# Loading one half of the partitions from GpSimd, the other from SP

## The chip, the cores and the metric

The kernel runs on one core of one Trainium2 chip. The metric is device time in microseconds. Five engines work side by side: TensorE (PE), VectorE (DVE), ScalarE (ACT), GpSimd (POOL) and SyncE (SP). Each works its own list of instructions in order, and semaphores tie them together. DMAs are issued by an engine into a queue and carried out by 16 DMA engines.

## The reference

Two layers over 4096 nodes of 128 features, with one adjacency matrix `adj` of 4096 x 4096 fp32 (64 MB), which is read once in each layer:

```python
sim = jnp.tanh(adj * simlar)            # layer 0, simlar is adj: tanh(adj^2)
new_adj = ...                           # its 350 largest entries in each row
h2 = jnp.tanh(h @ W_proj + b_proj)
feat = jax.nn.relu(new_adj @ (h2 @ W_gcn) + b_gcn)
x = layernorm(x + feat)
pos = (adj > 0) @ x;  neg = (adj < 0) @ x       # layer 1
node = concat(pos, neg) @ node_weight + node_bias * diag(adj)
edge = (adj @ x) @ edge_weight + edge_bias * diag(adj)
x = layernorm(x + node + edge)
```

The matrix is sparse and has no negative entries. The kernel counts the positive entries of each row and the negative ones while it works; where no row has over 350 positive entries, the selection changes nothing, and a general path at the end (under `when_failed`) is skipped.

## The kernel before

Both layers go through the rows of `adj` in 8 chunks of 512 rows (`CHUNKS`, `CH`). A chunk is 8.39 MB. It is cut by columns into 4 pieces (`PIECES`), and a piece into 2 halves of 4 blocks each (`HALVES`, `HB`), so a chunk has 8 halves (`HPC`).

The 4096 columns are dealt to the partitions in quarters: partitions 0 to 31 hold columns 0 to 1023, partitions 32 to 63 the next 1024, and so on, each partition every 32nd row of the chunk. A piece is 256 columns of each quarter. So `load_chunk` (L309 to L321, on SP) issues four DMAs for a piece, one for each quarter. Each fills 32 partitions of `a_rows` with 16 x 256 numbers, that is 512 KB in 512 runs of 1 KB (L320). There are 4 slots in `a_rows`, one for each piece of a chunk; a slot is free for the next chunk's piece when VectorE has turned its second half (layer 0: `turned`), or when ScalarE has counted it (layer 1: `counted`). Before the chunks, SP loads x in 8 groups (L304), and after chunk 0's loads some small things, the diagonal of `adj` among them (L330).

The way of a half in layer 0:

- VectorE waits until the piece has landed and transposes each 32 x 32 square, `a_cols<-a_rows`, 128 x 2048 (`turn`, L477). `a_cols` has 4 slots for halves; a slot is free when TensorE has used it.
- GpSimd squares the first two blocks in place (L296), ScalarE the other two (L405); then ScalarE takes the tanh of all four (L409).
- TensorE multiplies the four blocks into the chunk's sum, `acc<-a_cols,rhs` (L874). An fp32 product stands as two records in the trace, so a half is 8 records and a chunk 64.

Behind this the chunk before is finished: ScalarE's relu (L394), VectorE's addition of x (L547), TensorE's turn of `z_t` into rows after half 1 (L839), VectorE's layer norm in three parts after its transposes 5, 6 and 7, TensorE's turn back of the new x after half 5 (L848), ScalarE's copy (L388).

In layer 1 the chunks run backwards from the last, which is still in `a_rows`. VectorE transposes a half and makes a mask of it (`masks<-a_cols`, L657); TensorE does three products for each block (L932 to L934); ScalarE goes over each piece in `a_rows` twice to count (L433, L436), and GpSimd has nothing. Results go out by DMAs that ScalarE issues, on another queue than SP's.

The order of each engine's work is written out by hand in the functions below; nothing reorders it. `chunks(engine, body)` (L214) runs a body for chunk 0, in a loop for the chunks 1 to 6, and for the last.

Of the kernel before, what the change touches and what calls it, by code (L numbers as in the profile page):

```python
# [21 lines left out]
SQ = 32  # L22
# [9 lines left out]
def build(nc, x, adj, w_proj, b_proj, w_gcn, b_gcn, node_w, node_b, edge_w, edge_b, out):  # L32
# [4 lines left out]
    QUARTERS = P // SQ  # L37
    QUARTER = N // QUARTERS
    BLOCKS = N // P
    CH = 512  # L40
    CHUNKS = N // CH
# [3 lines left out]
    PIECES = 4  # L45
    PCOLS = QUARTER // PIECES
    HALVES = 2
    HB = PCOLS // HALVES // SQ
    SLOTS = 4
    HSLOTS = 4  # L50
    HPC = PIECES * HALVES
    LAST = (CHUNKS - 1, CHUNKS // 2 - 1, 1)
    SQ_POOL = HB // 2

# [6 lines left out]
    with ctx:  # L61
# [6 lines left out]
        def sem(name):  # L68
            return ctx.enter_context(nc.semaphore(name))
# [7 lines left out]
        a_rows = sb("a_rows", [P, SLOTS, ROWSETS, PCOLS])  # L77
# [38 lines left out]
                     to_cols[:, 0:PARTS[1][1] * F].rearrange("p (t f) -> p t f", f=F)]  # L116


        def half_in(slot, h):
            w = PCOLS // HALVES  # L120
            return a_rows[:, slot, :, h * w:(h + 1) * w].rearrange("p r (b j) -> p r b j", j=SQ)
# [37 lines left out]
        x_loaded = [sem(f"x_loaded{g}") for g in range(CHUNKS)]  # L159
        small_loaded = sem("small_loaded")  # L160
        wl1_loaded = sem("wl1_loaded")
        a_loaded = [sem(f"a_loaded{k}") for k in range(SLOTS)]
        zeroed = sem("zeroed")
        consts = sem("consts")
        staged = sem("staged")
# [11 lines left out]
        counted = sem("counted")  # L177
# [34 lines left out]
        def chunks(eng, body):  # L212


            body((0, 0, 0), None)
            with eng.Fori(0, (CHUNKS - 2) // 2) as pair:
                body((pair * 2 + 1, pair, 1), (pair * 2, pair, 0))
                body((pair * 2 + 2, pair + 1, 0), (pair * 2 + 1, pair, 1))
            body(LAST, (CHUNKS - 2, CHUNKS // 2 - 1, 0))

        def rows_of(chunk):


            c, q, parity = chunk
            return c * -1 + (CHUNKS - 1), q * -1 + (QUARTERS - 1), 1 - parity
# [8 lines left out]
        EVEN_FIRST = [*range(0, GROUPS, 2), *range(1, GROUPS, 2)]  # L234
# [49 lines left out]
        @block.gpsimd  # L284
        def _(pool):
            nc.gpsimd.memset(ident[:], 0.0).then_inc(zeroed, 1)
            nc.gpsimd.memset(ones[:], 1.0).then_inc(consts, 1)
            pool.wait_ge(zeroed, 1)
            nc.gpsimd.affine_select(out=ident[:], in_=ident[:], compare_op=ALU.not_equal, fill=1.0, base=0,
                                    pattern=[[-1, P]], channel_multiplier=1).then_inc(consts, 1)  # L290

            def layer0(chunk, before):
                for h in range(HPC):
                    part = a_cols[:, h % HSLOTS, 0:SQ_POOL, :]
                    pool.wait_ge(turned[0], chunk[0] * HPC + h + 1)
                    nc.gpsimd.tensor_tensor(part, part, part, ALU.mult).then_inc(squared_pool, 1)  # L296

            chunks(pool, layer0)

        @block.sync  # L300
        def _(sp):
            def load_x():
                for g in EVEN_FIRST:
                    sp.dma_start(xr[:, g * TILES:(g + 1) * TILES, :],  # L304
                                 x[g * CH:(g + 1) * CH, :].rearrange("(t p) f -> p t f", p=P))\
                        .then_inc(x_loaded[g], 16)

            load_x()

            def load_chunk(layer, c):  # L310
                r = c * -1 + (CHUNKS - 1) if layer == 1 else c
                for s in range(PIECES):

                    if layer == 0 and not is_first(c):
                        sp.wait_ge(turned[0], HPC * (c - 1) + HALVES * (s + 1))
                    if layer == 1:
                        sp.wait_ge(counted, PIECES * (c - 1) + s + 1)
                    for q in range(QUARTERS):
                        src = adj[bass.ds(r * CH, CH), q * QUARTER + s * PCOLS:q * QUARTER + (s + 1) * PCOLS]
                        sp.dma_start(a_rows[SQ * q:SQ * (q + 1), s, :, :],  # L320
                                     src.rearrange("(r i) k -> i r k", i=SQ)).then_inc(a_loaded[s], 16)  # L321

            load_chunk(0, 0)

            for k, b in enumerate((node_b, edge_b, b_gcn)):
                sp.dma_start(b_row[:, k, :], b.rearrange("(a f) -> a f", a=1)).then_inc(wl1_loaded, 16)
            sp.dma_start(w_pne[:, 0:2, :], node_w.rearrange("(s p) f -> p s f", p=P)).then_inc(wl1_loaded, 16)
            sp.dma_start(w_pne[:, 2, :], edge_w).then_inc(wl1_loaded, 16)
            with nc.allow_non_contiguous_dma(reason="the diagonal"):
                sp.dma_start(diag[:], bass.AP(adj.tensor, 0, [[N + 1, P], [P * (N + 1), ALL_TILES]]))\  # L330
                    .then_inc(wl1_loaded, 16)

            for layer in range(2):
                with sp.Fori(1, CHUNKS) as c:
                    load_chunk(layer, c)

            sp.wait_ge(stored[0], 16 * (CHUNKS // 2))
            sp.wait_ge(stored[1], 16 * (CHUNKS // 2 + 1))

            with when_failed(sp):  # L340
                load_x()

                def g_load0(t, q, s):
                    sp.wait_ge(g_tile_free, t + 1)
                    sp.dma_start(g_in, adj[bass.ds(t * P, P), :]).then_inc(g_loaded[0], 16)
                    sp.dma_start(g_x, x[bass.ds(t * P, P), :]).then_inc(g_loaded[0], 16)

                def g_load1(t, q, s):
                    sp.wait_ge(g_tile_free, t + ALL_TILES + 1)
                    sp.dma_start(g_in, adj[bass.ds(t * P, P), :]).then_inc(g_loaded[1], 16)  # L350
                    sp.wait_ge(normed, t + NORMS + ALL_TILES + 1)
                    sp.dma_start(out[bass.ds(t * P, P), :], g_out).then_inc(g_stored, 16)

                g_tiles(sp, g_load0)
                g_tiles(sp, g_load1)
                sp.wait_ge(g_stored, 16 * ALL_TILES)
# [106 lines left out]
        def _(dve):  # L463
            EARLY = 3

            def turn(layer, c, h):

                s, hs = h // HALVES, h % HSLOTS
                n = c * HPC + h
                if h % HALVES == 0 and not (layer == 1 and is_first(c)):  # L470
                    dve.wait_ge(a_loaded[s], 16 * QUARTERS * (c + layer * (CHUNKS - 1) + 1))

                if h >= HSLOTS or not is_first(c):
                    dve.wait_ge(half_used[layer], n + 1 - HSLOTS)
                elif layer == 1:
                    dve.wait_ge(half_used[0], HPC * CHUNKS + n + 1 - HSLOTS)
                nc.vector.transpose(half_out(hs), half_in(s, h % HALVES)).then_inc(turned[layer], 1)  # L477
                return n, hs
# [579 lines left out]
```

## Time and profile before

| | |
|---|---|
| median of 3 runs | 723.9 us |
| lowest, highest | 722.14, 725.73 us |
| profiled execution, its span | 724.8 us |
| TensorE busy | 635.2 us, 88% |
| VectorE, ScalarE busy | 492.6 and 450.0 us, 68% and 62% |
| GpSimd busy | 122.2 us, 17% |
| moved by DMA | 130.62 MB, 180 GB/s over the span |

For the profiled execution the page gives its span alone; what lies around it shows in no view. The span is 0.9 us above the median of the runs.

The page cuts the span into 40 slices of 18.1 us. Slices 1 to 19 are layer 0 (until 353 us), the rest layer 1. Busy shares of an engine are averages over stretches with different limits, so they are to be read by stretch. In the rows by stretch each engine has its busy us and, in brackets, its instructions. A DMA share above 1 means that the packets' times overlap on a DMA engine. Lines such as L477 are lines of the kernel before; the change moves most of them by 10 or 26.

### The profile page before, as it was taken

Reading aid. Unit: us, or ns where it says so; the run is one execution under the profiler, and the core shown is the slowest. Engines: PE = TensorE matmul, PEld = TensorE weight load, DVE = VectorE, ACT = ScalarE, POOL = GpSimd, SP = SyncE. Lnnn points to the kernel's source line nnn. Section 1 sums busy time; section 2 is a strip of 40 time slices with the busy share of each in tenths; the row PEclk is TensorE's granted clock in tenths of the full one; section 3 lists DMA queues with packets and bytes.
Section 4 is the critical chain, followed back from the end, with each engine's and each line's share of the span. In section 5 each row is a group of like instructions: output and inputs, shape, how many; then the busy total and the mean of one; then the engine's idle time right before and its main releaser. Section 6 shows DMA issues by size and latency. Waiting matters only on the chain.

```text
span 724.8 us, 6808 instructions
## 1 busy us (share of the span) xinstructions
PE 635.2 (88%) x2016; PEld 353.6 (49%) x2016; DVE 492.6 (68%) x689; ACT 450.0 (62%) x302; POOL 122.2 (17%) x71
## 2 busy tenths in 40 slices
PE   7866858698786869696999999999999999999994
PEld 4522323243333334242666555555555555555993
DVE  3454574857656675748856489797978778787854
ACT  2564556565666655665318996768678667658750
POOL 0234334343334443334000000000000000000000
PEclk9998989989898989899899999999999999999998
DMA  9999999999999999993002999999999999999000
GB/s 208 214 176 209 212 211 212 212 212 211 211 211 212 211 212 212 211 213 73 1 0 54 212 211 211 226 213 227 213 227 212 227 213 212 226 212 220 16 16 16
DMA packets 140312, 130.62 MB, mean 180 GB/s; under 512 B 8579, under 2 KB 140294, under 8 KB 140294
## 3 DMA queue, kind: packets, MB, share of 16 engines
q1 hardware_dynamic: 135478, 128.16, 93.1%
q10 hardware_dynamic: 4816, 2.23, 1.2%
q8 instruction: 10, 0.16, 0.1%
q14 instruction: 8, 0.07, 0.0%
HBM read 128.27 MB, written 2.10 MB: 180 GB/s over the span
## 4 chain that ended last, share of the span: by engine, by line
PE 46%; SPq 42%; DMA 4%; issue 3%; DVE 3%; ACT 2%; DVEq 0%
SPq L320 40%; PE acc L932 23%; PE acc L934 6%; PE acc L933 6%; DMA a_rows<-in_adj_dram 4%; PE stage L896 2%; PE stage L952 2%; PE acc L952 2%; PE acc L874 1%; DVE a_cols L477 1%; ACT a_rows L436 1%; ACT a_rows L433 1%; SPq L304 1%; PE stage L954 1%; PE acc L954 1%
## 5 line engine op out<-in xcount | busy, mean ns | idle before, releaser
L477 DVE STREAM_TRANSPOSE a_cols<-a_rows 128x2048 f32<-128x2048 f32 x128 | 293.0, 2303 | 163.2 <-DMA a_rows<-in_adj_dram 124.3
L874 PE MATMUL acc<-a_cols,rhs 128*128 128x512 f32 x512 | 243.6, 633 | 21.3 <-ACT a_cols L409 21.3
L932 PE MATMUL acc<-a_cols,rhs 128*128 128x512 f32 x448 | 229.0, 592 | 0.0
L933 PE MATMUL acc<-masks,pos_hi 128*128 128x512 f32 x224 | 178.5, 797 | 0.0
L874 PEld LDWEIGHTS acc<-a_cols,rhs 128*128 128x128 f32 x512 | 102.4, 205 | 151.8 <-issue 133.4
L433 ACT ACTIVATE a_rows<-a_rows 128x4096 f32<-128x4096 f32 x32 | 115.9, 3621 | 76.8 <-DVE a_cols L477 76.8
L296 POOL TENSOR_TENSOR a_cols<-a_cols 128x1024 f32<-128x1024 f32 x64 | 121.3, 1896 | 221.1 <-DVE a_cols L477 221.1
L409 ACT ACTIVATE a_cols<-a_cols 128x2048 f32<-128x2048 f32 x64 | 122.2, 1910 | 39.3 <-POOL a_cols L296 38.5
L405 ACT ACTIVATE a_cols<-a_cols 128x1024 f32<-128x1024 f32 x64 | 67.3, 1051 | 89.8 <-DVE a_cols L477 89.8
L436 ACT ACTIVATE a_rows<-a_rows 128x4096 f32<-128x4096 f32 x32 | 116.0, 3624 | 2.9
L932 PEld LDWEIGHTS acc<-a_cols,rhs 128*128 128x128 f32 x448 | 83.9, 189 | 19.3
L934 PE MATMUL acc<-masks,pos_lo 128*128 128x512 f32 x224 | 88.7, 396 | 0.0
L657 DVE TENSOR_SCALAR masks<-a_cols 128x2048 fp32r<-128x2048 f32 x64 | 78.5, 1227 | 2.2
L934 PEld LDWEIGHTS acc<-masks,pos_lo 128*128 128x128 f32 x224 | 42.4, 189 | 53.7 <-issue 53.7
L933 PEld LDWEIGHTS acc<-masks,pos_hi 128*128 128x128 f32 x224 | 42.2, 188 | 53.9 <-issue 53.9
L848 PE MATMUL to_cols<-ident,n_rows 128*128 128x128 f32 x32 | 8.4, 414 | 40.5 <-DVE n_rows L537 40.5
L848 PEld LDWEIGHTS to_cols<-ident,n_rows 128*128 128x128 f32 x32 | 5.5, 207 | 46.4 <-DVE n_rows L537 46.3
L532 DVE SCALAR_TENSOR_TENSOR root<-tmp,root 128x4 f32<-128x4 f32 (+1 forms) x51 | 19.0, 372 | 2.1 <-DVE tmp L531 0.4
L839 PE MATMUL to_rows<-ident,z_t 128*128 128x128 f32 x60 | 9.4, 280 | 12.3 <-DVE z_t L547 11.1
L952 PE MATMUL stage<-a_cols,rhs 128*128 128x256 f32 x64 | 19.1, 380 | 0.0
L952 PE MATMUL acc<-a_cols,rhs 128*128 128x256 f32 x64 | 19.0, 379 | 0.0
L547 DVE TENSOR_TENSOR z_t<-z_t,feat_t 128x512 f32<-128x512 f32 x8 | 5.5, 692 | 18.0 <-ACT z_t L394 18.0
(83 smaller groups left out, 322.7 us busy)
## 6 DMA issues: line engine op xcount, KB each, us to landing
a_rows<-in_adj_dram SPq DMA_DIRECT2D x240, 512.0 KB, 14.5
early<-in_x_dram SPq DMA_DIRECT2D x8, 256.0 KB, 6.1
out_dram<-n_rows ACTq DMA_DIRECT2D x7, 256.0 KB, 9.9
out_dram<-n_rows ACTq DMA_DIRECT2D x2, 128.0 KB, 1.8
w_pne<-n_L_gnn_node_weight_dram SPq DMA_DIRECT2D x1, 128.0 KB
w_pg<-in_L_gnn_W_proj_dram ACTq DMA_DIRECT2D x1, 64.0 KB, 2.7
w_pg<-in_L_gnn_W_gcn_dram ACTq DMA_DIRECT2D x1, 64.0 KB, 3.2
w_pne<-n_L_gnn_edge_weight_dram SPq DMA_DIRECT2D x1, 64.0 KB
```

The lines of the kernel that those rows point to most:

```text
L296: nc.gpsimd.tensor_tensor(part, part, part, ALU.mult).then_inc(squared_pool, 1)
L320: sp.dma_start(a_rows[SQ * q:SQ * (q + 1), s, :, :], src.rearrange("(r i) k -> i r k", i=SQ)).then_inc(a_loaded[s], 16)
L405: nc.scalar.activation(a_cols[:, hs, SQ_POOL:, :], a_cols[:, hs, SQ_POOL:, :], ACT.Square)\
L409: nc.scalar.activation(a_cols[:, hs, :, :], a_cols[:, hs, :, :], ACT.Tanh)\
L433: nc.scalar.activation(piece, piece, ACT.Sign, accum_out=signs[:, bass.ds(col, 1)])\
L436: nc.scalar.activation(piece, piece, ACT.Relu, scale=-1.0, accum_out=negs[:, bass.ds(col, 1)]).then_inc(counted, 1)
L477: nc.vector.transpose(half_out(hs), half_in(s, h % HALVES)).then_inc(turned[layer], 1)
L657: nc.vector.tensor_scalar(masks[:, hs, :, :], a_cols[:, hs, :, :], 0.0, None, ALU.is_gt)\
L874: last = nc.tensor.matmul(acc[parity][:], rhs[:, b, :], a_cols[:, h % HSLOTS, k, :], start=(b == 0), stop=(b == BLOCKS - 1))
L932: nc.tensor.matmul(acc[parity][:], rhs[:, b, :], cols, start=(b == 0), stop=False)
L933: nc.tensor.matmul(acc[parity][:], pos_hi[:, b, :], mask, start=False, stop=False)
L934: last = nc.tensor.matmul(acc[parity][:], pos_lo[:, b, :], mask, start=False, stop=(b == BLOCKS - 1))
```

## The change

Of the four loads of a piece, SP issues the two for partitions 0 to 63 (`SP_QUARTERS`), and GpSimd the two for partitions 64 to 127 (`POOL_QUARTERS`), on its own queue and with semaphores of their own (`high_loaded`). VectorE waits for both before the first transpose of a piece. The loads themselves are as they were, in size and in number.

GpSimd issues chunk 0's 8 loads when the last group of x has landed. In layer 0 it issues the two loads of the next chunk's piece when both halves of the piece are turned, and only then squares the second half. In layer 1 it waits for `counted` as SP does.

```diff
+    SP_QUARTERS = range(QUARTERS // 2)
+    POOL_QUARTERS = range(QUARTERS // 2, QUARTERS)
...
+        def quarter_of(s, q):
+            return a_rows[SQ * q:SQ * (q + 1), s, :, :]
+
+        def quarter_in(r, s, q):
+            src = adj[bass.ds(r * CH, CH), q * QUARTER + s * PCOLS:q * QUARTER + (s + 1) * PCOLS]
+            return src.rearrange("(r i) k -> i r k", i=SQ)
...
+            def load_piece(r, s):
+                for q in POOL_QUARTERS:
+                    pool.dma_start(quarter_of(s, q), quarter_in(r, s, q)).then_inc(high_loaded[s], 16)
+
             def layer0(chunk, before):
                 for h in range(HPC):
                     part = a_cols[:, h % HSLOTS, 0:SQ_POOL, :]
                     pool.wait_ge(turned[0], chunk[0] * HPC + h + 1)
+                    if h % HALVES == HALVES - 1 and chunk is not LAST:
+                        load_piece(chunk[0] + 1, h // HALVES)
                     nc.gpsimd.tensor_tensor(part, part, part, ALU.mult).then_inc(squared_pool, 1)
 
+            def layer1(chunk, before):
+                if chunk is LAST:
+                    return
+                for s in range(PIECES):
+                    pool.wait_ge(counted, chunk[0] * PIECES + s + 1)
+                    load_piece(rows_of(chunk)[0] - 1, s)
+
+            pool.wait_ge(x_loaded[EVEN_FIRST[-1]], 16)
+            for s in range(PIECES):
+                load_piece(0, s)
             chunks(pool, layer0)
+            chunks(pool, layer1)
...
-                    for q in range(QUARTERS):
-                        src = adj[bass.ds(r * CH, CH), q * QUARTER + s * PCOLS:q * QUARTER + (s + 1) * PCOLS]
-                        sp.dma_start(a_rows[SQ * q:SQ * (q + 1), s, :, :],
-                                     src.rearrange("(r i) k -> i r k", i=SQ)).then_inc(a_loaded[s], 16)
+                    for q in SP_QUARTERS:
+                        sp.dma_start(quarter_of(s, q), quarter_in(r, s, q)).then_inc(a_loaded[s], 16)
...
-                    dve.wait_ge(a_loaded[s], 16 * QUARTERS * (c + layer * (CHUNKS - 1) + 1))
+                    dve.wait_ge(a_loaded[s], 16 * len(SP_QUARTERS) * (c + layer * (CHUNKS - 1) + 1))
+                    dve.wait_ge(high_loaded[s], 16 * len(POOL_QUARTERS) * (c + layer * (CHUNKS - 1) + 1))
```

GpSimd's instructions in chunk 0 of layer 0 before, from the mask of the identity on; in brackets the semaphore that a row waits for:

```order
L289 AFFINE_SELECT ident<-ident 128x128
L296 TENSOR_TENSOR a_cols<-a_cols 128x1024 [waits turned_l0] x8
```

And now, the same place, until chunk 0's fourth square:

```order
L299 AFFINE_SELECT ident<-ident 128x128
L304 DMA a_rows<-in_adj_dram 32x16x256 [waits x_loaded7]
L304 DMA a_rows<-in_adj_dram 32x16x256 x7
L312 TENSOR_TENSOR a_cols<-a_cols 128x1024 [waits turned_l0]
L304 DMA a_rows<-in_adj_dram 32x16x256 [waits turned_l0]
L304 DMA a_rows<-in_adj_dram 32x16x256
L312 TENSOR_TENSOR a_cols<-a_cols 128x1024
L312 TENSOR_TENSOR a_cols<-a_cols 128x1024 [waits turned_l0]
L304 DMA a_rows<-in_adj_dram 32x16x256 [waits turned_l0]
L304 DMA a_rows<-in_adj_dram 32x16x256
L312 TENSOR_TENSOR a_cols<-a_cols 128x1024
```

Eight issues stand ahead of the first square now, and two ahead of every second one.

SP's instructions in layer 0's loop for one piece before:

```order
L320 ISA [waits turned_l0]
L320 DMA a_rows<-in_adj_dram 32x16x256
L320 ISA
L320 DMA a_rows<-in_adj_dram 32x16x256
L320 ISA
L320 DMA a_rows<-in_adj_dram 32x16x256
L320 ISA
L320 DMA a_rows<-in_adj_dram 32x16x256
L315 REGISTER_ALU
```

And now:

```order
L346 ISA [waits turned_l0]
L346 DMA a_rows<-in_adj_dram 32x16x256
L346 ISA
L346 DMA a_rows<-in_adj_dram 32x16x256
L342 REGISTER_ALU
```

SP has half the loads behind the same wait; its order is otherwise the same.

## Rows read from the trace of the kernel before

**Rows 1.** The page's span, and the rate of DMA in 40 slices.
```profile
span 724.8 us, 6808 instructions
...
GB/s 208 214 176 209 212 211 212 212 212 211 211 211 212 211 212 212 211 213 73 1 0 54 212 211 211 226 213 227 213 227 212 227 213 212 226 212 220 16 16 16
```

**Rows 2.** Stretches: us; busy PE, PEld, DVE, ACT, POOL; PE's clock; DMA share; GB/s.
```profile
100.00:300.00 200.00, 156.67 (x360) 69.06 (x360) 130.33 (x175) 122.53 (x92) 76.94 (x41) 0.91 1.13 212
410.00:640.00 230.00, 228.72 (x707) 130.89 (x705) 185.72 (x240) 168.22 (x92) 0.00 (x0) 1.00 1.13 218
414.00:424.00 10.00, 8.72 (x29) 4.85 (x28) 7.59 (x5) 9.89 (x7) 0.00 (x0) 1.00 1.12 212
```

**Rows 3.** Groups: busy us, mean ns of one, idle before it and its releaser.
```profile
L477 DVE STREAM_TRANSPOSE a_cols<-a_rows 128x2048 f32<-128x2048 f32 x128 | 293.0, 2303 | 163.2 <-DMA a_rows<-in_adj_dram 124.3
...
L296 POOL TENSOR_TENSOR a_cols<-a_cols 128x1024 f32<-128x1024 f32 x64 | 121.3, 1896 | 221.1 <-DVE a_cols L477 221.1
L409 ACT ACTIVATE a_cols<-a_cols 128x2048 f32<-128x2048 f32 x64 | 122.2, 1910 | 39.3 <-POOL a_cols L296 38.5
L405 ACT ACTIVATE a_cols<-a_cols 128x1024 f32<-128x1024 f32 x64 | 67.3, 1051 | 89.8 <-DVE a_cols L477 89.8
```

**Rows 4.** TensorE's timeline, chunk 0's end and one chunk: start us, us, what.
```profile
59.60 10.14 PE L874 MATMUL acc<-a_cols,rhs 128*128 128x512 f32 x16 [2.92 <-ACT a_cols L409]
...
203.55 0.66 PE L839 MATMUL to_rows<-ident,z_t 128*128 128x128 f32 x4 [2.25 <-DVE z_t L547]
204.05 7.03 PE L874 MATMUL acc<-a_cols,rhs 128*128 128x512 f32 x16
212.05 7.13 PE L874 MATMUL acc<-a_cols,rhs 128*128 128x512 f32 x16 [0.97 <-ACT a_cols L409]
224.97 1.12 PE L848 MATMUL to_cols<-ident,n_rows 128*128 128x128 f32 x4 [5.78 <-DVE n_rows L537]
...
243.21 0.66 PE L839 MATMUL to_rows<-ident,z_t 128*128 128x128 f32 x4 [1.59 <-DVE z_t L547]
```

**Rows 5.** The chain of waits at the start: start us, us, SP's issues by line.
```profile
0.75 0.46 SPq L304
...
5.81 1.47 SPq L304
...
7.32 0.67 SPq L320
...
22.90 3.11 SPq L320
```

**Rows 6.** SP's lines: L304's landing; L320's issues (ns, least/median/most) and landing.
```profile
DMA to landing us min/median/max: 3.6/6.1/7.6
...
L320 SPq DMA_DIRECT2D a_rows<-in_adj_dram x240: 316/2164/8272, 7.3 to 661.4; - x120
...
DMA to landing us min/median/max: 4.4/14.5/16.3
```

**Rows 7.** DMA queues (packets, MB, share) from 8-11, 100-300 and 456.0-457.4 us.
```profile
q1 hardware_dynamic: 1480, 0.81, 118.8%
...
q1 hardware_dynamic: 42610, 42.32, 112.6%
...
q1 hardware_dynamic: 321, 0.32, 80.0%
q10 hardware_dynamic: 252, 0.12, 33.9%
```

**Rows 8.** Timelines of VectorE and GpSimd in layer 0.
```profile
218.10 1.92 POOL L296 TENSOR_TENSOR a_cols<-a_cols 128x1024 f32<-128x1024 f32 x1 [5.91 <-DVE a_cols L477]
218.30 1.74 DVE L532 SCALAR_TENSOR_TENSOR root<-tmp,root 128x4 f32<-128x4 f32 x1
...
227.96 1.89 POOL L296 TENSOR_TENSOR a_cols<-a_cols 128x1024 f32<-128x1024 f32 x1 [2.33 <-DVE a_cols L477]
230.15 1.89 POOL L296 TENSOR_TENSOR a_cols<-a_cols 128x1024 f32<-128x1024 f32 x1 [0.30 <-DVE a_cols L477]
```

More of the change, by code:

```diff
@@ L162, in build @@
         a_loaded = [sem(f"a_loaded{k}") for k in range(SLOTS)]
+        high_loaded = [sem(f"high_loaded{k}") for k in range(SLOTS)]
         zeroed = sem("zeroed")
```

## The prediction

> **What bounds the kernel now.** I read the page first: in its 40 slices GB/s sits at 211 to 212 all through the first layer [rows 1]. Then the busy time by stretch: from 100 to 300 us TensorE works 156.67 of 200 us at a granted clock of 0.91, VectorE, ScalarE and GpSimd less; in layer 1 (410 to 640) TensorE works 228.72 of 230 us at 1.00 [rows 2]. The groups say who waits: VectorE's transposes stand 124.3 us behind DMA, GpSimd's squares 221.1 us behind the transposes [rows 3]. So layer 0 is bound by the adjacency loads and layer 1 by TensorE. A chunk is 16 loads of 512 KB, 8.39 MB; at 212 GB/s that is 39.6 us, and the timeline of TensorE has the same: its turn of z_t starts at 203.55 and again at 243.21, a period of 39.66 us [rows 4]. Whatever the change gives must come from layer 0's period, seven of them from the end of chunk 0.
>
> Next question: what holds the loads at 212? Three candidates. (a) SP's issuing: 2.16 us in the median for a load, back to back, is 512 KB / 2.16. But in the chain the first x loads (also 512 packets) cost SP 0.46 us at first, the first adjacency load 0.67, and only later ones 2 to 3.11 [rows 5]; over all 240 the least is 316 ns [rows 6]. An issue that can take 0.3 us and takes 2.2 is held back by a full queue; landing 14.5 us after issue, six loads later, says the same. (b) The DMA engines or HBM as such. Against it: from 456.0 to 457.4 us a store ran on the other queue; together they moved 0.32 + 0.12 MB in 1.4 us, 314 GB/s, and the load queue lost nothing: 0.32 MB / 1.4 us = 229 GB/s. From 8 to 11 us, while x was arriving into all 128 partitions in packets of half the size, 0.81 MB went in 3 us, 270 GB/s [rows 7]. (c) The shape: each adjacency load fills 32 partitions, and the queue works them off in order. Its packets took 1.126 x 16 x 200 us / 42610 = 85 ns each; beside x's, 1.188 x 16 x 3 us / 1480 = 39 ns for half the bytes [rows 7]. I hold (c) likeliest: something on the way into those partitions is full. The rows can't say where, since no load of partitions 64 to 127 ever runs beside one of 0 to 63.
>
> The Trainium skill, SBUF — State Buffer, "Door 1: The DMA port swizzle", names it: partitions 0 to 63 reach only eight of sixteen ports, 64 to 127 the other eight, with about 218 GB/s for eight. The 212 here fits that. By this alone two streams would carry 424 and the loads would stop bounding. A rule on the other side stands among the rivals.
>
> **The change part by part.**
>
> 1. Bytes, packets and loads stay: 16 loads a chunk, 8 from SP, 8 from GpSimd. SP's share of issuing falls to half; it was waiting on its queue, so that gives nothing by itself.
>
> 2. Two streams, to different halves of the partitions. Bounds from rows: no more than 212, a period of 39.6; or twice 212, 19.8. Between lie 270 (31.1 us) and 314 (26.7 us). I take 290 to 314, nearest to the stretch in which two queues did run together: 27 to 29 us. Then the loads are late no more, and the next server decides.
>
> 3. TensorE is next: two runs of 16 records (7.03 and 7.13 us) are half a chunk, so 28.3 us, and the two turns 0.66 and 1.12: 30.1 us a chunk at full clock [rows 4]. ScalarE has 8 x (1.05 + 1.91) plus about 1.2, 25 us [rows 3]; VectorE 130.33 of 200, 26 us a chunk [rows 2].
>
> 4. GpSimd gets 8 issues a chunk, and between them its 8 squares. Squares that had no wait came 2.19 us apart (227.96, 230.15) [rows 8], 17.5 us a chunk. What an issue costs GpSimd, call it T, no row shows: it issues none. Bounds by SP's: 0.32 us (queue empty) and 3.11 us (a long one behind a full queue) [rows 5, 6]; the longest of all, 8.272 us, is the first behind the diagonal's tiny packets and no price of issuing. Between ends a factor of ten apart the nearest rows are SP's issues into a queue that isn't full, 0.46 to 0.67 us for as many packets; I take about three times that, T = 1.6 us, an estimate, because GpSimd is the slow engine of this kernel (1.89 us for a square of 1024 elements, where ScalarE takes 1.05) [rows 3]. The Trainium skill, DMA: Bandwidth & Descriptors, "SWDGE vs HWDGE vs iDMA", has GpSimd's own cores compute what SP gets from hardware, and gives first bytes after about 1 and 0.6 us; at that ratio T would be near 1, TensorE's 30.1 us would decide, and the time would be about 650 us. By 1.6 us GpSimd's period is 17.5 + 12.8 + about 0.3 = 30.6 us.
>
> The issues are queued ahead of the odd half's square on the same engine: ScalarE's tanh of that half waits for it, and TensorE behind. This costs latency, 3.2 us a piece. With four half slots the transposes can run two pieces ahead, so it is hidden as long as the period covers it; without that cover it would be 4 x 3.2 = 12.8 us a chunk.
>
> Loads 27 to 29, TensorE 30.1, GpSimd 30.6: three servers this close don't interlock perfectly. I add 1.4 us: a period of 32.0. Gain 7 x (39.66 - 32.0) = 53.6 us.
>
> 5. Chunk 0. GpSimd starts issuing when the last x group has landed, 5.81 + 7.6 = 13.4 us [rows 5, 6], and has 8 issues before its first square: to 26.2 us, against 25.5 before, so nothing lost. Then four times (4.4 + 3.2) us, 56.6; tanh 1.9 and TensorE's 3.6 behind it: chunk 0 ends at 62.1 us. Before it ended at 59.60 + 10.14 = 69.7 [rows 4]. Gain 7.6 us.
>
> 6. Layer 1. TensorE never waits but for 1.28 us between 414 and 424, behind the first refill [rows 2]: gain 1.3. GpSimd has 12.8 us of issues in over 40, with nothing else to do.
>
> 7. The waits. VectorE's doubled wait costs an instruction a piece. SP loses none of its own waits; GpSimd's wait for `counted` delays nobody else.
>
> Sum: 53.6 + 7.6 + 1.3 = 62.5, so 724.8 - 62.5 = 662.3 us for the profiled span. That span is 0.9 us above the median of the runs (723.9); I forecast 661 us. Its own ends: with T near 0.32 GpSimd is no server, the period is 30.1 and chunk 0 gains 11: 724 - 67 - 11 - 1 = 645. With T = 2.16, SP's median, the period is 35.1 and chunk 0 ends 2 us later: 724 - 32 + 2 - 1 = 693.
>
> **The rivals.**
>
> A. *The streams share one limit.* If what is full is common to both halves, the sum stays between 212 and the 227 GB/s that the slices show where stores run along [rows 1]: period 39.6 to 37.0, time 705 to 724, say 714. For it: the DMA engines' share is above 1 all along [rows 2], so no engine is ever free; against it: the 314 GB/s [rows 7], although the store writes the other way. The Trainium skill has this rule: DMA: Bandwidth & Descriptors, "Rules for kernel authors", says of two transfers to disjoint partition halves "Don't bother — they serialize", and SBUF — State Buffer, "Can I just issue two DMAs to hit both halves?", measured 6% more. That would be 225 GB/s, a period of 37.3 and 707 us.
>
> B. *GpSimd's issuing becomes the bound: slower.* Place: the square of the odd half, behind two issues. The period is 17.9 + 8T, and chunk 0 ends at 36.5 + 16T. Sum of gains: 7 x (21.8 - 8T) + (33.2 - 16T) + 1.3, which is nothing at T = 2.6 us. With T = 3.11 the period is 42.8 and the time 724 + 22 + 17 - 1 = 762 us. For it: no row has GpSimd's price, and it is slow in its squares [rows 3]; against it: 2.6 us is four to five times what SP needs for as many packets.
>
> C. *VectorE and GpSimd get in each other's way in layer 1.* They do today: a 4-element VectorE operation that takes 0.163 us in the median took 1.74, from 218.30 until GpSimd's square (218.10 + 1.92) was over [rows 8]. If each of 56 masks waited out an issue of 1.6 us, VectorE would have 90 us more, where its slack is 44.3 of 230 us [rows 2], 58 over the some 300 us of those chunks: 32 us late, 693 us. For it: the collision above; against it: issues fill 12.8 of 42 us, so most masks meet none.
>
> **How the numbers follow.** Forecast (both streams side by side, T up to 2.2) 0.62, its own range 645 to 693; A 0.15; B 0.17; C or a T between 2.2 and 2.6, 0.06. The range reaches from 640 (the free end, less a few us of clock that an unbroken TensorE would get back) to 724, which takes in A and C and leaves out B. A measurement of this kernel can tell about 0.5%, 3.6 us, from no change: faster 0.62 + 0.06 + two thirds of A = 0.78, same 0.05, slower 0.17.
>
> **What the profile after would show.** Right: GB/s in layer 0 of 255 to 275 (8.39 MB in 32 us), TensorE above 9 tenths there and its granted clock up from 0.91, VectorE's wait for DMA gone to below 30 us, landing below 14.5 us. Layer 0 would end near 290 us, not 353. GpSimd's issues would stand between its squares at about 1.6 us each. Wrong: GB/s at 212 to 227 (A); or VectorE waiting for a DMA of GpSimd's queue while SP's has landed, and ScalarE's tanh waiting for squares, TensorE's period above 36 (B); or masks longer than 1.23 us in layer 1 with TensorE idle (C).

## The result

| | before | after |
|---|---|---|
| median of 5 runs | 722.14 us | 694.14 us |
| lowest, highest | 717.3, 725.73 | 693.2, 697.25 |
| profiled execution, its span | 724.8 us | 695.6 us |
| ratio of the times, 95% interval | | 0.962 (0.958 to 0.967) |

The change makes the kernel 28 us faster. The forecast was 661 us, 62 us faster: the sign was right, the size was not, and 694 lies inside the wide range but a microsecond beyond the forecast's own, 645 to 693. Ratios here and below are to the kernel before, from undisturbed executions alone (one of the run with mixed quarters and two of the run with GpSimd's issues behind the square were over 1.5% slower and are left out).

The page after has GpSimd's queue as a software queue beside SP's. Each moves half the matrix, SP's in packets of 1 KB, GpSimd's in larger ones. Each load ends with 16 tiny packets, 1920 for its 120 loads; the other 15360 of 17280 carry the 62.92 MB, 4096 bytes each:

```profile
span 695.6 us, 6849 instructions
...
GB/s 208 248 258 183 205 250 232 243 227 241 231 240 228 240 229 241 228 73 0 1 1 219 242 246 245 246 252 224 205 217 193 200 208 193 206 202 176 0 16 17
...
q1 hardware_dynamic: 72118, 65.23, 47.9%
q0 software_dynamic: 17280, 62.92, 38.1%
```

Layer 0 no longer stands at 212 GB/s [rows 1]; from the sixth slice on it swings between 227 and 250. By stretch, with the columns of [rows 2]:

```profile
100.00:280.00 180.00, 157.15 (x371) 69.45 (x369) 140.98 (x172) 122.25 (x91) 103.67 (x81) 0.94 1.08 236
410.00:640.00 230.00, 230.00 (x709) 131.71 (x707) 188.46 (x253) 163.22 (x88) 29.69 (x44) 1.00 1.01 216
```

236 GB/s make a chunk of 8.39 MB last 35.5 us. TensorE's turns of `z_t` say the same: 90.12 us for chunk 0 and 303.25 for chunk 6, six periods of 35.5 (before 83.64 and 322.3, 39.8). The chain of waits has one load of SP's in each period, here from 142.17 and from 177.81 us:

```profile
142.17 26.29 DMA a_rows<-in_adj_dram
...
177.81 26.54 DMA a_rows<-in_adj_dram
```

So the loads still set the pace, although VectorE waits for them only 6.3 us between 100 and 280 us (44.0 before): the rest of each period is VectorE's work on the piece, until its slot is free for SP's next load. Below is TensorE's timeline; [rows 4] had 59.60 + 10.14 for the end of chunk 0 and 39.66 for a period. The turn of a chunk's `z_t` stands behind the first two halves of the next chunk, so the line at 62.84 ends chunk 0 and the one at 80.41 is chunk 1's:

```profile
62.84 7.42 PE L900 MATMUL acc<-a_cols,rhs 128*128 128x512 f32 x16 [1.95 <-ACT a_cols L434]
80.41 9.87 PE L900 MATMUL acc<-a_cols,rhs 128*128 128x512 f32 x16 [10.15 <-ACT a_cols L434]
90.12 0.60 PE L865 MATMUL to_rows<-ident,z_t 128*128 128x128 f32 x4
...
194.09 0.66 PE L865 MATMUL to_rows<-ident,z_t 128*128 128x128 f32 x4
...
230.76 0.66 PE L865 MATMUL to_rows<-ident,z_t 128*128 128x128 f32 x4
```

Chunk 0 ends at 70.3 us (69.7 before); then TensorE waits 10.15 us for chunk 1's first piece. The 29.2 us of the span come together from four places: 6.5 lost up to the turn of chunk 0 (83.64 to 90.12), of which 0.5 by the end of chunk 0 and 6.0 behind it; 25.5 gained over the next six periods (238.7 to 213.1), 9.1 in the last (34.71 to 25.64), and 1.1 in layer 1 (367.8 to 366.7).

GpSimd's issues are cheap, and the landings are uneven. The lines of the two issuing statements, as [rows 6] (ns, least, median, most; then us from issue to landing):

```profile
L304 POOL DMA_DIRECT2D a_rows<-in_adj_dram x120: 650/650/1629, 13.7 to 631.7; - x120
...
DMA to landing us min/median/max: 6.9/10.7/25.5
...
L346 SPq DMA_DIRECT2D a_rows<-in_adj_dram x120: 316/702/9551, 7.4 to 631.0; - x120
...
DMA to landing us min/median/max: 4.3/18.3/37.8
```

Where both queues have work (151.7 to 157.7 us) and where SP is alone (178.5 to 183.5), the queue rows say why:

```profile
q0 software_dynamic: 338, 1.25, 79.5%
q1 hardware_dynamic: 336, 0.33, 25.5%
...
q1 hardware_dynamic: 987, 0.98, 113.0%
```

338 packets to 336: the DMA engines take the queues in turn, packet by packet. GpSimd's packet is four times as long, so it gets 1.25 MB of 1.58 in 6 us, 208 GB/s, and SP 55. The 208 is all that GpSimd's queue moves when it runs alone (209, below), and the turns tie SP to a quarter of it. Then GpSimd's loads of the piece are done and SP, alone, does 0.98 MB in 5 us, 196 GB/s. Worked out for a chunk: 20.2 us for GpSimd's 4.19 MB, in which SP moves 1.1, and 15.7 us for SP's other 3.1, 35.9 us in all where 35.5 were measured. Over the run VectorE waited 46.6 us for SP's loads and 12.9 for GpSimd's: the starved queue is the late one.

### The profile page after: what moved, and what is told of

The parts are those of the page before. It is cut to its first block, busy times and chain, and to the rows that moved or that the text cites. A ratio compares the mean times of both kernels' runs of the same rounds, so it can differ in the third digit from the quotient of the medians.

```text
span 695.6 us, 6849 instructions
## 1 busy us (share of the span) xinstructions
PE 628.3 (90%) x2016; PEld 351.7 (51%) x2016; DVE 502.5 (72%) x689; ACT 449.0 (65%) x302; POOL 202.7 (29%) x191
## 3 DMA queue, kind: packets, MB, share of 16 engines
q0 software_dynamic: 17280, 62.92, 38.1%
## 4 chain that ended last, share of the span: by engine, by line
PE 61%; DMA 20%; DVE 8%; issue 5%; SPq 3%; POOL 1%; ACT 1%; DVEq 0%; POOLq 0%; ACTq 0%
PE acc L958 28%; DMA a_rows<-in_adj_dram 20%; PE acc L900 9%; PE acc L960 8%; PE acc L959 7%; DVE a_cols L503 3%; SPq L346 3%; DVE root L558 2%; PE stage L922 2%; PE stage L978 2%; PE acc L978 2%; SPq L331 1%; POOL a_cols L312 1%; DVE tmp L557 1%; PE to_rows L865 1%
## 5 line engine op out<-in xcount | busy, mean ns | idle before, releaser
L503 DVE STREAM_TRANSPOSE a_cols<-a_rows 128x2048 f32<-128x2048 f32 x128 | 293.6, 2304 | 123.5 <-DMA a_rows<-in_adj_dram 59.5
L900 PE MATMUL acc<-a_cols,rhs 128*128 128x512 f32 x512 | 238.4, 624 | 23.7 <-ACT a_cols L434 23.5
L958 PE MATMUL acc<-a_cols,rhs 128*128 128x512 f32 x448 | 229.0, 592 | 0.0
L304 POOL DMA_DIRECT2D a_rows<-in_adj_dram x120 | 80.7, 676 | 337.4 <-ACT a_rows L461 274.1
L959 PE MATMUL acc<-masks,pos_hi 128*128 128x512 f32 x224 | 178.5, 797 | 0.0
L573 DVE TENSOR_TENSOR z_t<-z_t,feat_t 128x512 f32<-128x512 f32 x8 | 10.0, 1248 | 20.5 <-ACT z_t L419 20.5
## 6 DMA issues: line engine op xcount, KB each, us to landing
a_rows<-in_adj_dram SPq DMA_DIRECT2D x120, 512.0 KB, 18.3
a_rows<-in_adj_dram POOLq DMA_DIRECT2D x120, 512.0 KB, 10.7
```

The source lines that it names most:

```text
L304: pool.dma_start(quarter_of(s, q), quarter_in(r, s, q)).then_inc(high_loaded[s], 16)
L900: last = nc.tensor.matmul(acc[parity][:], rhs[:, b, :], a_cols[:, h % HSLOTS, k, :], start=(b == 0), stop=(b == BLOCKS - 1))
L958: nc.tensor.matmul(acc[parity][:], rhs[:, b, :], cols, start=(b == 0), stop=False)
L959: nc.tensor.matmul(acc[parity][:], pos_hi[:, b, :], mask, start=False, stop=False)
```

## The experiments

**Loads alone.** 16 stretches without any arithmetic, each of the same 512 KB loads ("wide": loads of 2 MB into all 128 partitions), each waiting for the one before.

```diff
+        PHASES = [dict(sp=(0, 1, 2, 3)), dict(sp=(0, 2, 1, 3)), dict(sp=(0, 1), pool=(2, 3)),
+                  dict(sp=(0, 1), act=(2, 3)), dict(sp=(0,), act=(1,)), dict(sp=(0,), act=(2,)),
+                  dict(sp=(0,), pool=(1,)), dict(sp=(0,), pool=(2,)), dict(pool=(0, 1, 2, 3)), ...
+                  dict(sp="wide"), dict(sp=(0, 2), act=(1, 3)), ...]   # quarters of the partitions
```

> Loads alone, no arithmetic and no x: 16 stretches, each waiting for the one before, with the same 512 KB loads into 32 partitions (four quarters, 0 to 3, of the partitions; 0 and 1 are partitions 0 to 63). Theory R (turns): a DMA engine takes one packet in turn from each queue that has work and hardly overlaps them; GpSimd's packets hold 4096 bytes, SP's 1024, so GpSimd gets four fifths. Theory L (limit of the partitions): each half of the partitions takes 212 to 218 GB/s, and the halves add up. Theory S (shared): one limit for everything. SP alone, quarters 0 1 2 3: all say 212 GB/s. SP low and ACT high, equal packets: L says 350 to 424, S says 212 to 230, R alone says nothing but an equal split. SP quarter 0 and ACT quarter 1 (same half): L says 212, and beside it SP 0 and ACT 2 (other half) 350 to 424; S and R say the same for both. SP low and GpSimd high: R says 268 while both run, of that GpSimd 209, then SP alone at about 200. GpSimd alone: R and S give about 212; if its larger packets are cheaper, more. One load over all 128 partitions from SP: L says 350 or more, S 212. SP alone in the order 0 2 1 3: L with strict order says 212 to 230.

Measured, a row for each of the nine stretches written out, then "wide" and the last one written out. Columns: stretch, its length, GpSimd's busy time, PE's clock, DMA share, GB/s.

```profile
2.00:42.00 40.00, 0.00 (x0) 1.00 1.10 209
43.70:81.70 38.00, 0.00 (x0) 1.00 1.10 220
83.50:118.90 35.40, 4.30 (x7) 1.00 1.06 236
120.70:146.50 25.80, 0.00 (x0) 1.00 1.05 325
148.30:168.90 20.60, 0.00 (x0) 1.00 1.07 203
170.80:184.20 13.40, 0.00 (x0) 1.00 1.03 311
185.90:206.30 20.40, 1.87 (x3) 1.00 1.02 203
208.10:225.80 17.70, 1.65 (x3) 1.00 1.01 235
228.20:267.90 39.70, 8.61 (x14) 1.00 1.01 209
...
394.20:421.40 27.20, 0.00 (x0) 1.00 0.97 307
422.80:460.10 37.30, 0.00 (x0) 1.00 1.09 224
```

Read in pairs. SP quarter 0 with ScalarE quarter 1, both below partition 64: 203. With quarter 2, above: 311. So the limit of about 210 belongs to a half of the partitions, and two halves nearly add up: 325 for SP low and ScalarE high, 307 for one load over all 128 partitions. Nothing shared by all DMA engines stops at 212. But with GpSimd in ScalarE's place the same split gives 236 (the kernel's own number), GpSimd beside one quarter of SP's in the other half 235 and in the same half 203. GpSimd's queue alone is as fast as SP's, 209. And two queues by themselves give little: in the last row SP and ScalarE have equal packets, but both go through the halves in the same order, and the rate is 224.

**Packet lengths.** Loads alone again.

```diff
+        # (quarters in order, runs of KB, loads that a quarter of a piece is cut into)
+        PHASES = [..., dict(sp=((0, 2, 1, 3), 1, 4)), ..., dict(sp=((0, 1), 1, 1), pool=((2, 3), 1, 1)),
+                  dict(sp=((0, 1), 2, 1), pool=((2, 3), 2, 1)), dict(sp=((0, 1), 4, 1), pool=((2, 3), 4, 1)),
+                  dict(sp=((0, 1), 1, 1), act=((2, 3), 1, 1)), dict(sp=((0, 1), 4, 1), act=((2, 3), 4, 1)),
+                  dict(sp=((0, 1), 4, 1), act=((2, 3), 1, 1))]
```

> Loads alone again, each stretch 8.39 MB in 11 stretches; what varies is the length of the runs (1, 2 or 4 KB, which is SP's packet) and into how many loads a quarter of a piece is cut. Theory T (turns and lengths: while SP's packet is 1 KB and GpSimd's 4 KB, four fifths of the time all 16 DMA engines write to the half that GpSimd serves, two by two at one rate of 212 GB/s; with equal packets half of them write to each half): SP low and GpSimd high with 1 KB runs 237 GB/s as measured; with 2 KB runs 260 to 290; with 4 KB runs, where both packets are 4 KB, 310 to 330, with equal shares. Rival G (GpSimd's queue is slow in itself, by its descriptors or where they lie): 237 to 250 GB/s in all three. SP low and ACT high: 325 at 1 KB and at 4 KB by T; with 4 KB runs on SP and 1 KB on ACT, T says 240 to 260 with unequal shares again, without GpSimd; G says 325. One queue, order 0 2 1 3: 220 at full loads; cut into 4 or 8, the queue changes halves every 8 or 4 packets of an engine: if engines drift out of step the rate goes up to 240 to 300, if they stay in step it stays at 220.

The stretches written out, in their order:

```profile
84.10:118.10 34.00, 0.00 (x0) 1.00 1.02 246
...
222.80:258.70 35.90, 4.33 (x7) 1.00 1.04 233
260.20:291.60 31.40, 3.61 (x7) 1.00 1.01 266
293.30:324.70 31.40, 3.36 (x7) 1.00 1.00 266
326.60:352.50 25.90, 0.00 (x0) 1.00 1.05 323
354.10:384.40 30.30, 0.00 (x0) 1.00 0.98 275
386.10:422.60 36.50, 0.00 (x0) 1.00 1.03 229
```

The last row reproduces the loss without GpSimd: 4 KB packets on SP beside 1 KB on ScalarE give 229, where equal 1 KB packets give 323. So unequal packets are enough. The theory missed one thing: equal packets of 4 KB were to give 310 or more and gave 266 with GpSimd, 275 with ScalarE. Length costs by itself, and GpSimd's queue as such little (266 to 275, 3%). Why long packets in step share the two halves worse was not measured. A single queue cut into loads of 128 KB, halves alternating, gives 246; cut into 64 KB it fell to 138, at SP's issuing: 128 loads in 60.5 us, 0.47 us each.

**The order of the quarters, one queue** (the kernel before):

```diff
-                    for q in range(QUARTERS):
+                    for q in (0, 2, 1, 3):
```

> The kernel before, SP alone issuing, with the four loads of a piece in the order 0, 2, 1, 3 of the quarters, so that neighbours in the queue go to different halves of the partitions. If engines spread over two neighbouring loads, the rate rises above 212 GB/s and the time falls below 722 us (at 236 GB/s, as after the change, to about 694). If the queue is worked off load by load in step, no change: 720 to 724 us. My guess: 215 to 225 GB/s, 705 to 722 us.

Measured: 713.54 us, ratio 0.985 (0.977 to 0.992), within the guess; from 100 to 280 us it moves 216 GB/s (212 before). Neighbouring loads overlap a little.

**Quarters mixed over the queues** (the changed kernel):

```diff
-    SP_QUARTERS = range(QUARTERS // 2)
-    POOL_QUARTERS = range(QUARTERS // 2, QUARTERS)
+    SP_QUARTERS = (0, 2)
+    POOL_QUARTERS = (1, 3)
```

> The changed kernel with the quarters dealt otherwise: SP issues 0 and 2, GpSimd 1 and 3, so each queue serves both halves of the partitions. If the gain comes from the two halves of the partitions running side by side, it shrinks: at worst to 212 GB/s, 722 us. If it comes from having two queues, or from GpSimd's larger packets, it stays at about 236 GB/s and 694 us. And SP, left alone at a piece's end, would alternate between halves.

Measured: 710.07 us, ratio 0.979 (0.969 to 0.988), against 0.962 (0.958 to 0.967). A good half of the change's gain remains. In this deal each queue changes halves from load to load, so the two queues can be in different halves only for a part of the time; how large a part was not measured.

**Three quarters for GpSimd:**

```diff
+    SP_QUARTERS = (0,)
+    POOL_QUARTERS = (1, 2, 3)
```

> The changed kernel with SP issuing quarter 0 alone and GpSimd quarters 1, 2 and 3. If turns between packets of 4096 and 1024 bytes give GpSimd 209 and SP 58 GB/s, a piece now takes 1.5 MB / 209 = 7.5 us on one queue and 0.5 MB / 58 = 9 us on the other, near 8.2 us with the one alone at the end, against 8.8 in the changed kernel: a chunk of 33 us instead of 35.3, seven of them 16 us less: 678 us. If the total is bound at 236 GB/s by anything shared, 694 us stays. GpSimd's 12 issues at 0.65 us are 8 us a chunk beside 17.5 of squares and don't bound.

Measured: 706.37 us, ratio 0.978 (0.971 to 0.985): worse, 28 us above the expected 678. The periods were as expected, 32.3 to 33.2 us but for one of 36.8 (TensorE's turns at 136.18 and 168.60), but chunk 0's turn came at 103.9 us instead of 90.1. Chunk 0 itself ended as early as in the changed kernel; then TensorE waited for chunk 1's first piece:

```profile
93.83 10.21 PE L900 MATMUL acc<-a_cols,rhs 128*128 128x512 f32 x16 [23.88 <-ACT a_cols L434]
```

The queues from 60 to 70 us show what held SP's part of that piece:

```profile
q0 software_dynamic: 595, 2.17, 100.1%
q1 hardware_dynamic: 594, 0.00, 6.7%
```

SP's 594 packets carry next to nothing: they are the diagonal of `adj`, 4096 single numbers, which stand in SP's queue ahead of chunk 1's loads. Each takes its turn with a packet of 4 KB. With one queue, before, they were through in about 5 us (49 to 54.5 us: 4164 packets under 512 bytes); here they take over 30.

**ScalarE issues the high half from chunk 1 on (e4):**

```diff
                     nc.scalar.activation(a_cols[:, hs, :, :], a_cols[:, hs, :, :], ACT.Tanh)...
+                    if h % HALVES == HALVES - 1 and chunk is not LAST:
+                        load_piece(chunk[0] + 1, h // HALVES)    # act.dma_start
```

> The changed kernel with ScalarE issuing the loads of partitions 64 to 127 from chunk 1 on (GpSimd still those of chunk 0): after its tanh of a piece's second half in layer 0, after its count in layer 1. Its packets are 1 KB like SP's. Theory T says the loads reach 325 GB/s as in the loads-alone run, a chunk's loads take 25.8 us and layer 0 is bound by TensorE and what lies between the engines: a period of 31 to 33 us instead of 35.6, seven of them 18 to 32 us less than 694: 662 to 676 us. If ScalarE is held at an issue by a full queue (2 us each, 8 a chunk), it has 25 + 16 = 41 us of work and the period is 39 or more: 715 us or more. A rival in which only GpSimd's work was in the way (its squares and issues) says 33 us too, but with GB/s alternating as after the change.

Measured: 660.61 us, ratio 0.913 (0.908 to 0.919), just under the range expected. The turns stand at 206.11 and 236.24, a period of 30.13 us: TensorE's 28.3 + 1.8 of the prediction.

**Half of each run loaded (e5).** In layer 0 from chunk 1 on, the other half keeps chunk 0's numbers.

```diff
+        load_piece(chunk[0] + 1, h // HALVES, PCOLS // 2)         # SP's loads likewise
```

> The changed kernel, in layer 0 from chunk 1 on with only the first half of each 1 KB run loaded (the other half of the slot keeps chunk 0's numbers), same number of loads, runs and issues: what layer 0 costs with the same instructions when loads don't bound it. The prediction had 30.1 us for TensorE and 32.0 for the period with waits in between. If the period falls to 30 to 33 us, the loads alone are what the change left; if it stays near 35.6, it is GpSimd's issues ahead of the squares or the waits between engines. I expect 31.5 us, and about 665 us in all.

Measured: 672.13 us in one run; period 34.0 us, not 31.5. Even with the loads at 113 GB/s the changed kernel's own instructions don't reach TensorE's 30.1. GpSimd's timeline beside VectorE's shows where:

```profile
189.33 2.31 DVE L504 STREAM_TRANSPOSE a_cols<-a_rows 128x2048 f32<-128x2048 f32 x1
...
192.31 1.31 POOL L304 DMA_DIRECT2D a_rows<-in_adj_dram  x2 [4.30 <-DVE a_cols L504]
193.63 3.75 POOL L312 TENSOR_TENSOR a_cols<-a_cols 128x1024 f32<-128x1024 f32 x2
```

The transpose ends at 191.64 and the square of that half starts at 193.63: 0.67 us until the issues, 1.31 for the two, and only then the square. With ScalarE issuing, transpose (until 190.58) and square touch:

```profile
188.27 2.31 DVE L506 STREAM_TRANSPOSE a_cols<-a_rows 128x2048 f32<-128x2048 f32 x1
...
190.66 1.89 POOL L311 TENSOR_TENSOR a_cols<-a_cols 128x1024 f32<-128x1024 f32 x1 [3.71 <-DVE a_cols L506]
```

It settled a second thing. Chunk 0 is loaded in full here as in the changed kernel. VectorE's transposes of its last piece and of chunk 1's first, in the changed kernel, then in this one:

```profile
56.41 4.51 DVE L503 STREAM_TRANSPOSE a_cols<-a_rows 128x2048 f32<-128x2048 f32 x2 [4.87 <-DMA a_rows<-in_adj_dram]
74.08 4.50 DVE L503 STREAM_TRANSPOSE a_cols<-a_rows 128x2048 f32<-128x2048 f32 x2 [13.16 <-DMA a_rows<-in_adj_dram]
```
```profile
51.89 4.50 DVE L504 STREAM_TRANSPOSE a_cols<-a_rows 128x2048 f32<-128x2048 f32 x2 [2.18 <-DMA a_rows<-in_adj_dram]
60.94 8.89 DVE L504 STREAM_TRANSPOSE a_cols<-a_rows 128x2048 f32<-128x2048 f32 x4 [4.55 <-DMA a_rows<-in_adj_dram]
```

Only chunk 1's loads were made smaller, and chunk 0's last piece comes 4.5 us earlier. So in the changed kernel chunk 1's loads delay chunk 0's: GpSimd is already loading for the next chunk (its first issue for it is at 32.10 us) while SP's loads for this one get the small share. Chunk 1's first piece comes 13 us earlier, in part because it is half as long itself.

**ScalarE issues all of the high half,** chunk 0's too; GpSimd issues nothing.

```diff
+                    if firsts:                                   # before each of ScalarE's first 8
+                        s, q = firsts.pop(0)
+                        act.dma_start(quarter_of(s, q), quarter_in(0, s, q)).then_inc(high_loaded[s], 16)
```

> As e4, and ScalarE issues chunk 0's loads of partitions 64 to 127 too, one ahead of each of its first eight instructions, so that GpSimd issues nothing. In the changed kernel chunk 0 ended 6 us later than before, since SP's loads starve beside GpSimd's 4 KB packets. With equal packets piece 0 lands first, piece 1 next: chunk 0 ends by 70 us instead of 76; total 6 to 10 us below e4. If ScalarE is held at the issues while x is being transformed, chunk 0 is later by up to 8 us and the time is that of e4 or worse.

Measured: 656.64 us, ratio 0.907 (0.901 to 0.913): the best version, 37 us below the changed kernel. The gain over the former is 4 us where 6 to 10 were expected, and the intervals of the two overlap. Chunk 0 ends at 60.6 us, earlier than expected, but its turn is at 80.1: TensorE waits 9.87 us for chunk 1's first piece, since the diagonal is in the way here too (from 44 to 48 us SP's queue moves 773 packets with no bytes to speak of, ScalarE's 776 full ones). In layer 0 TensorE works at the full clock, and from chunk 1 on an issue costs ScalarE 0.38 us in the median, no wait for a full queue:

```profile
100.00:250.00 150.00, 142.51 (x360) 64.11 (x359) 127.51 (x171) 120.92 (x91) 75.70 (x40) 1.00 1.11 279
...
L381 ACTq DMA_DIRECT2D a_rows<-in_adj_dram x112: 317/382/590, 32.2 to 588.9; - x112
```

279 GB/s is demand now, 8.39 MB in a period of 30.1 us, and not a limit: loads alone reach 325, and TensorE is the bound.

**GpSimd's issues behind the square,** first with full loads, then with the half runs of e5 above:

```diff
-                    if h % HALVES == HALVES - 1 and chunk is not LAST:
-                        load_piece(chunk[0] + 1, h // HALVES)
                     nc.gpsimd.tensor_tensor(part, part, part, ALU.mult).then_inc(squared_pool, 1)
+                    if h % HALVES == HALVES - 1 and chunk is not LAST:
+                        load_piece(chunk[0] + 1, h // HALVES)
```

> The changed kernel with GpSimd's two issues behind the square of the odd half instead of ahead of it. In the run with half of each run loaded the period of layer 0 was 34.0 us, though loads moved only 113 GB/s, against 30.1 with ScalarE issuing; so GpSimd's work costs up to 4 us a chunk. Theory Q (the place: the odd half's square starts 2.0 us after its transpose, and the four half slots don't cover it): here the loads bound again at 35.6 us, or a little below, 690 to 694 us, since loads are the later of the two; only the half-load run would show it in full. Theory T alone (loads bound): no change, 694 us. If the time falls by more than 10 us, GpSimd's place was the bound and not the loads.

> As e5 (half of each run loaded in layer 0 from chunk 1 on), with GpSimd's issues behind the odd half's square. By Q the period falls from 34.0 us to 30 to 31.5, near ScalarE's 30.1. If what costs is GpSimd's descriptor work as such (its 5.2 us a chunk, or the time in which it keeps VectorE waiting), wherever it stands, it stays at 33 to 34.

Measured: 695.99 us, ratio 0.958 (0.954 to 0.962) with full loads, which the intervals don't separate from the change's 0.962. With half runs 654.25 us in one run (672.13 with the issues ahead), turns at 168.85 and 198.95, a period of 30.1 instead of 34.0. So the place of the issues costs 4 us a chunk, and it is hidden behind loads of 35.5. The rival in which GpSimd's work alone was in the way falls with this.

**Chunk 0 by SP alone:**

```diff
-            pool.wait_ge(x_loaded[EVEN_FIRST[-1]], 16)
-            for s in range(PIECES):
-                load_piece(0, s)
...
-                    for q in SP_QUARTERS:
+                    for q in range(QUARTERS) if is_first(c) else SP_QUARTERS:
```

> The changed kernel with chunk 0 loaded by SP alone, in the old order, and GpSimd issuing from chunk 1 on. In the changed kernel TensorE's turn for chunk 0 is at 90.1 us, before at 83.6: 6.5 us lost at the start, by the theory because SP's loads of the first piece share with GpSimd's 4 KB packets, one to four. Then it is near 84 here, the periods stay at 35.6, and the time is 5 to 7 us below 694: 688 us. If the loss has another cause (the diagonal's small packets, GpSimd's work), it stays at 90 and 694 us.

Measured: 700.49 us, ratio 0.966 (0.962 to 0.969), not separated from the change's 0.962; chunk 0's turn at 88.9 us. The theory in this form fell: sharing inside chunk 0's first pieces isn't the loss. It agrees with the finding of the half runs: SP now has all of chunk 0 in its queue, GpSimd's loads for chunk 1 start as soon as piece 0 is turned, and chunk 0's last piece is turned at 64.99 us, 11.8 later than in the kernel before (53.17). What the diagonal adds to the loss at the start was not run apart: no run moved its load.

**One queue, cut finely** (the kernel before, no second queue):

```diff
+                    for pair in ((0, 2), (1, 3)):
+                        for u in range(CUTS):                     # 4 loads of 128 KB for each of 512
+                            for q in pair:
+                                ... sp.dma_start(...)
```

> The kernel before, SP alone issuing, each load cut into four of 128 KB, in the order of quarters 0, 2, 0, 2, ... and then 1, 3, 1, 3, ... Loads alone moved 247 GB/s that way (220 uncut in the order 0 2 1 3, 210 in the old order). If the theory of the two halves carries over, with one queue and no GpSimd, a chunk takes 34.0 us instead of 39.7: seven of them and the start 40 us less than 724: 684 us, below the changed kernel's 694. With 64 issues a chunk at 0.5 us SP is at its limit of 32 us; if it becomes late in layer 1, 700 us.

Measured: 673.3 us, ratio 0.925 (0.920 to 0.931): better than expected, and 21 us below the changed kernel with SP alone:

```profile
100.00:280.00 180.00, 158.38 (x389) 70.78 (x388) 132.80 (x174) 128.35 (x96) 79.63 (x42) 0.96 1.09 245
```

A little more than the change's 236, and chunk 0's turn at 72.5 us instead of 90.1. That fits the two findings on the start: with one queue no load for chunk 1 overtakes chunk 0's, and the diagonal shares with nobody (2561 packets in 2 us, from 44 to 46).

## Why the prediction was wrong

- *What bounds the kernel (right).* Candidate (c), the shape of a load, holds: 203 with both streams in one half, 311 in two, 307 for loads over all partitions. Layer 1 gave 1.1 us where 1.3 were taken.
- *Step 2, the rate of two streams (the step that failed).* It took 290 to 314 GB/s from a stretch in which a store ran along, and from it concluded that "the loads are late no more". Measured: 263 while both run, 236 on average, so a load period of 35.5 us instead of 27 to 29, and the loads remained the bound. The halves do add up (325, not quite twice 209) with equal packets; GpSimd's packets are 4 KB, which no row of before showed, and queues are served packet by packet. A row of a 512-byte store beside 1 KB loads said nothing on that. Over seven periods this is 19 us: 53.6 forecast, 34.6 measured from turn to turn.
- *Step 4, GpSimd's price and place.* T was 0.65 us, not 1.6: by the formula 17.5 + 8 x 0.65, 22.7 us a chunk, far from a bound. Yet the claim that four half slots hide the issues was wrong: with loads out of the way the period was 34.0 with the issues ahead of the square, 30.1 behind it. It cost nothing that shows here, since the loads took longer still.
- *Step 3, TensorE's 30.1 us (right)*: 30.13 where nothing else bound. The 1.4 us added for waits wasn't needed.
- *Step 5, chunk 0 (wrong, with the other sign).* Its end was forecast at 62.1 us and came at 70.3 (69.7 before), 8.2 us off. The working counted GpSimd's issues and not which loads would land first. Another 6.0 us were lost behind it, for which no step had a term: chunk 1's first piece was turned at 74.08 us instead of 65.95. SP's part of it stood behind the rest of chunk 0 and behind the diagonal, all with the small share. Together 14 us, which with the 19 of step 2 make the miss of 33 (a gain of 62.5 forecast, 29.2 measured).
- *Luck.* That the forecast's upper end, 693, and rival C's 693 lie beside the measured 694 bears nothing out: the one was for issues of 2.16 us, the other for slow masks in layer 1, and neither was there.
- *Signs.* GB/s, 236, lay between the 255 to 275 of the forecast and the 212 to 227 of A. VectorE's wait for DMA was 59.5 us where less than 30 was the sign, the median landing 18.3 us for SP and 10.7 for GpSimd around 14.5.
- *Rivals.* A was nearest in place: the loads stay the bound; 236 GB/s lies beyond its 227, and its reason, one limit for both halves, is refuted by 325. The Trainium skill's rule against two transfers to disjoint halves (SBUF — State Buffer, "Can I just issue two DMAs to hit both halves?", 6% more) gave 707 us. Here GpSimd's stream brought 13% (from 209 alone to 236) and ScalarE's 56% (to 325), so with equal packets the rule doesn't hold in this case. B fell with T. C: masks stayed at 1.23 us and TensorE in layer 1 at 230.00 of 230; what the two engines' collisions did cost is in layer 0, where VectorE's addition of x took 1.25 us on average instead of 0.69 (and 0.69 again with ScalarE issuing).

## What to carry to other kernels

A queue full of loads that all go to one half of the partitions runs at that half's rate, about 210 GB/s here; put partitions 0 to 63 and 64 to 127 in flight together, by two queues with equal packets (SP and ScalarE, 325), by loads over all 128 partitions where the layout allows them (307), or by small alternating loads in one queue (246). Before a second queue is added, compare the packets of the two: the one with longer packets takes the larger share, and whoever waits for both waits for the other. And ask what the faster queue does next: a prefetch for the next chunk can overtake the rest of this one. Look last for tiny packets in either queue: the loads behind them wait until each has had its turn.

## What the runs showed of the hardware that was not expected

- Of runs of 1 KB GpSimd's queue made 4096-byte packets, SP's and ScalarE's 1 KB ones; alone both move 209 to 210 GB/s.
- An issue of 512 runs costs GpSimd 0.65 us, ScalarE 0.38 in the median and 0.32 at the least, as SP.
- Turns go by packets and not by bytes: with three quarters on GpSimd, 594 packets of single numbers in SP's queue took as long as 595 of 4 KB in GpSimd's, 10 us.
- Longer packets were not better: 323 GB/s with 1 KB on both hardware queues, 275 with 4 KB, 229 with one of each.
